# Score pairs in groups of two with a borrowed hidden bank, the second token transpose in two banks, and the norm of batch 1 moved ahead

## The reference

```python
x = x + xattn(layernorm(x), ctx, ctx)          # block-banded softmax, blocks of 64, out @ Wo.T
xn = layernorm(x)
top1 = argmax(softmax(xn @ gate_w.T))          # one of two experts per token
routed = sum_e relu(mask_e * xn @ w1[e] + b1[e]) @ w2[e] + b2[e]
x = x + routed + relu(xn @ sw1 + sb1) @ sw2 + sb2
```

## Time and profile before

| | us |
|---|---|
| median of 3 runs (944.99 to 947.7) | 946.83 |
| the profiled execution | 948.77 |
| its span | 946.6 |
| PE busy in the span | 807.7 (85%) |
| DVE, ACT, POOL busy | 598.4, 493.3, 420.3 |

### The profile page before, as it was taken

How to read it: one execution, slowest core, us unless ns; L and a number is a source line. 1 busy time by engine, 2 the same in 40 slices (tenths; PEclk the granted TensorE clock), 3 DMA queues, 4 the chain that set the end, 5 groups by cost and what they waited for, 6 DMA issues and landing times.

```text
span 946.6 us, 23198 instructions
## 1 busy us (share of the span) xinstructions
PE 807.7 (85%) x7862; PEld 670.6 (71%) x7862; DVE 598.4 (63%) x1226; ACT 493.3 (52%) x1108; POOL 420.3 (44%) x773
## 2 busy tenths in 40 slices
PE   3277877899998999898999989898989899988984
PEld 3146656586877868685968778686869596868884
DVE  3767584676758575776767575757577676646331
ACT  2373444436465555546464646455564646465542
POOL 3644324334344453635445544445363554455401
PEclk8587998979999999999999999999999999999998
DMA  8657232244435244344454453534434444414720
GB/s 269 172 150 252 78 102 67 76 137 142 151 110 185 88 147 149 107 148 136 135 153 144 128 172 95 172 110 133 152 115 137 152 133 137 142 46 134 253 83 23
DMA packets 97386, 128.17 MB, mean 135 GB/s; under 512 B 14655, under 2 KB 82623, under 8 KB 97088
## 3 DMA queue, kind: packets, MB, share of 16 engines
q1 hardware_dynamic: 89760, 107.89, 37.3%
q0 software_dynamic: 6624, 18.95, 5.9%
q10 hardware_dynamic: 960, 0.79, 0.4%
HBM read 90.80 MB, written 37.04 MB: 135 GB/s over the span
## 4 chain that ended last, share of the span: by engine, by line
PE 58%; DVE 15%; DMA 12%; ACT 6%; SPq 3%; issue 3%; POOL 1%; ACTq 1%; POOLq 0%; DVEq 0%
PE hid L502 19%; PE acc L671 13%; PE nd L596 10%; DVE T L1144 5%; DMA QP<-scratch_m 5%; PE work L580 4%; DMA scratch_m<-mT 3%; PE work L624 3%; PE work L502 2%; PE work L555 2%; DVE nmax L1125 2%; PE work L610 2%; DVE T L1141 2%; ACT h L925 1%; DVE Xs L1078 1%
## 5 line engine op out<-in xcount | busy, mean ns | idle before, releaser
L1404 POOL TENSOR_TENSOR hl<-h,hh 128x256 fp32r<-128x256 f32 x228 | 169.0, 744 | 351.2 <-ACT hh L925 351.1
L908 ACT ACTIVATE PT<-work 128x512 f32<-128x512 f32 x256 | 139.3, 600 | 58.4 <-PE work L580 55.8
L1144 DVE RECIPROCAL T<-nd 128x256 f32<-128x256 f32 x64 | 112.1, 1752 | 77.8 <-PE nd L596 74.0
L925 ACT ACTIVATE h<-hid,bias 128x256 f32<-128x256 f32 x144 | 69.0, 480 | 117.1 <-PE hid L502 117.1
L502 PE MATMUL hid<-Xs,W 128*128 128x256 f32 x816 | 115.1, 296 | 10.8 <-DVE Xs L1078 10.8
L502 PEld LDWEIGHTS hid<-Xs,W 128*128 128x128 f32 x816 | 105.1, 199 | 17.7 <-issue 10.8
L671 PE MATMUL acc<-w_hi,hh 128*128 128x256 f32 (+1 forms) x528 | 110.7, 292 | 0.0
L671 PE MATMUL acc<-w_lo,hh 128*128 128x256 f32 (+1 forms) x528 | 105.4, 281 | 0.0
L502 PE MATMUL hid<-Xr,W 128*128 128x256 f32 x768 | 105.3, 287 | 0.0
L596 PE MATMUL nd<-PT,V 128*32 128x256 f32 x1024 | 83.3, 398 | 25.4 <-DVE T L1146 22.5
L1125 DVE TENSOR_REDUCE nmax<-work 128x8 f32<-128x512 f32 x128 | 82.3, 685 | 35.1 <-PE work L555 35.0
(11 more groups left out here) (184 smaller groups left out, 1511.5 us busy)
## 6 DMA issues: line engine op xcount, KB each, us to landing
W<-w1q SPq DMA_DIRECT2D x64, 512.0 KB, 5.6
KP<-scratch_k SPq DMA_DIRECT2D x192, 64.0 KB, 2.3
QP<-scratch_q SPq DMA_DIRECT2D x180, 64.0 KB
scratch_k<-T SPq DMA_DIRECT2D x16, 512.0 KB, 3.5
scratch_q<-T SPq DMA_DIRECT2D x16, 512.0 KB, 3.3
yt<-yq SPq DMA_DIRECT2D x17, 260.0 KB, 2.8
xt<-xq SPq DMA_DIRECT2D x17, 256.0 KB, 3.8
xin<-x SPq DMA_DIRECT2D x16, 256.0 KB, 3.8
```

Of the source, the lines that this page charges most:

```text
L908: nc.scalar.activation(PT[:, j % 4].rearrange("p t q -> p (t q)"), work[:, BANK[("st", j)], :], ACT.Exp).then_inc(sem["exp_done"], 1)
L925: last = nc.scalar.activation(dst, hid[:, u % 2, a, :], ACT.Relu, bias=bias[:, 2 * u + a:2 * u + a + 1])
L1144: nc.vector.reciprocal(T[:, p, :], nd[:, p % 2, 1, :]).then_inc(sem["inverted"], 1)
L1404: nc.gpsimd.tensor_tensor(R(hl[:, u % 2, a]), h32[:, u % 2, a], hh[:, u % 2, a], ALU.subtract).then_inc(sem["hl_done"], 1)
```

## The change

- **Groups of two pairs.** `scores_t` of two pairs run back to back, then a fill, then both `values`. A group has four score jobs but `work` three banks; the fourth job goes into a half of `hid` (`score_bank`, `SPARE`), and waits there for the ReLU of the unit that lay in it (`relued`). Now the odd pair of each group is guessed, and the fills are one to a group: `shared_down` 3, `tile_up` 1, `tile_down` 0, `tile_up` 2. On ACT each group is four exponentials, in the first two groups a ReLU of the tile, then the guess.
- **x2T in two banks.** The token transposes of channel half 0 go to `work`, of half 1 to `hid`; each half has its own semaphore step, ACT and DVE split each half, and `shared_up` 0 waits for the second half only in its middle.
- **Shared units one place later.** `shared_down` 0 moves behind visit 2, 1 behind visit 3, 2 behind `tile_tokens`, 3 into the first group; ACT's ReLU of unit 3 moves behind the copy of the maxima, and DVE's `finish_shared` behind the next query projection.
- **attention_out** is done by channel half: 32 products of 64 columns in place of 16 of 128; the first half waits for four divides only.
- **Start.** Loads of batch 1 stand ahead of the key and query round trips, its statistics and norm ahead of the first maxima, the first weight splits of ACT ahead of its query loads.
- **Iterations 1 and 2**: ACT's `table_relu` moves from ahead of the last guess to behind it.
- **Tail.** The tile transposes of the last batch come two units later on PE, and SP reads the two row numbers before it waits for the padding.

```diff
-FILLED = {0: ("up", 1), 2: ("down", 0), 4: ("up", 2)}
-GUESSED_EARLY, GUESSED = (1, 3, 5, 7), (2, 3, 6, 7)
+FILLED = {1: ("up", 1), 2: ("down", 0), 3: ("up", 2)}
+GROUPS = PAIRS // 2
+SPARE = (1, 0, 0, 1)
+GUESSED_EARLY, GUESSED = (1, 3, 5, 7), (1, 3, 5, 7)
...
+        def score_bank(j):
+            if j % 4 == 3:
+                return flat(hid[:, SPARE[j // 4]])
+            return work[:, BANK["st", j], :]
+        def relued(i, group):
+            if type(i) is int and i == 0:
+                return None
+            if type(i) is int and i < 3:
+                return shared_unit(i - 1, UNITS - 1)
+            if group == 0 and type(i) is int and i == BATCH - 1:
+                return tile_unit(i - 2, 1)
+            if group == 0:
+                return shared_unit(i - 1, UNITS - 1)
+            return tile_unit(i - 2, SPARE[group])
+        def x2T_chunk(c):
+            return work[:, BANK["x2T", 0], 0:SEQ] if c == 0 else hid[:, 1, 0, :]
...
+            load_x(1)
+            load_ctx(1)
             bounce(0, "k_lo", kn, scratch_k, "first_k_bounced")
...
-            load_ctx(1)
-            load_x(1)
             iteration(0, False, False, True)
...
+            rows = [sp.value_load(left[0:1, e:e + 1], min_val=0, max_val=QROWS - TILE) for e in range(2)]
             for u in range(UNITS):
...
             sp.wait_ge(sem["padded"], 64)
-            rows = [sp.value_load(left[0:1, e:e + 1], min_val=0, max_val=QROWS - TILE) for e in range(2)]
...
             def scores_t(i, p, more):
-                banks = [claim(i, ("st", 2 * p + s), more) for s in range(2)]
+                banks = [score_bank(j) if j % 4 == 3 else claim(i, ("st", j), more) for j in (2 * p, 2 * p + 1)]
+                if p % 2:
+                    free = relued(i, p // 2)
+                    if free is not None:
+                        pe.wait_ge(sem["relu_done"], 2 * free + 2)
+                    if p > 1:
+                        pe.wait_ge(sem["exp_done"], HEADS * i + 2 * p - 2)
...
-                pe.wait_ge(sem["t_done"], PAIRS * (i + 1))
...
+                for c in range(DC):
+                    pe.wait_ge(sem["t_done"], PAIRS * i + 4 * c + 4)
+                    for r in range(NBLK):
+                        queries = slice(BLOCK * r, BLOCK * r + BLOCK)
+                        for q in range(4):
+                            mm = nc.tensor.matmul(bank[32 * q:32 * q + 32, c, queries], hsum[:, r, :],
+                                                  T[:, 4 * c + q, queries], start=True, stop=True)
...
+                if type(i) is not int or i > 0:
+                    pe.wait_ge(sem["relu_done"], 2 * last_odd(i) + 2)
+                transposes(bank, xhat2, "x2T_full", apart=hid[:, 1, 0, :])
...
                     ranks(n, claim(i, ("rk", 0), tile=tile))
-                    shared_down(n, 0)
                 visit(i, 2, more)
                 if shared:
+                    shared_down(n, 0)
                     shared_up(n, 2)
+                visit(i, 3, more)
+                if shared:
                     shared_down(n, 1)
-                visit(i, 3, more)
                 if tile:
                     shared_up(n, 3)
-                    shared_down(n, 2)
                 maxima(i)
...
-                    shared_down(n, 3)
+                    shared_down(n, 2)
...
-                scores_t(i, 0, more)
-                for p in range(PAIRS):
-                    if more or p != 0:
-                        fill(n, m, tile, p, expert)
-                    if p + 1 < PAIRS:
-                        scores_t(i, p + 1, more)
-                    values(i, p)
+                for group in range(GROUPS):
+                    scores_t(i, 2 * group, more)
+                    scores_t(i, 2 * group + 1, more)
+                    if more or group > 1:
+                        fill(n, m, tile, group, expert)
+                    values(i, 2 * group)
+                    values(i, 2 * group + 1)
...
                 high(i, "mT_full", work[:, BANK[("mT", 0)], 0:P], mT[:, 0, :], "mT_hi")
+                if tile:
+                    shared_relu(n, UNITS - 1)
...
+                for group in range(GROUPS):
+                    for j in range(4):
+                        exps(i, 4 * group + j)
+                    if tile and more and group < 2:
+                        tile_relu(m, group)
...
+                    guess_inverse(i, 2 * group + 1)
+                    if shared and not tile and group == 3:
                         table_relu(i - 1)
...
+            norm1_stats(1)
             for n in range(EARLY_PIECES):
                 if by_vector(n):
                     split_low(n)
+            norm1_apply(1)
             for j in range(4):
                 maximum(0, j)
```

More of the change, by code:

```diff
@@ L646, in ranks, with up @@
                                  skip_group_check=True).then_inc(sem["rk_full"], 1)
-            def up(g, u, weights, tokens):
+            def up(g, u, weights, tokens, second=None):
                 if type(g) is not int or g >= 2:
@@ L654, in up @@
                                        [(weights[:, u, 0, c, cols], weights[:, u, 1, c, cols]) for c in range(DC)],
-                                       [(tokens[:, 0, c, :], tokens[:, 1, c, :]) for c in range(DC)])
+                                       [(tokens[:, 0, c, :], tokens[:, 1, c, :]) for c in range(DC)],
+                                       second if a == 0 else None)
                 mm.then_inc(sem["hid_full"], 1)
@@ L767, in iteration @@
                 if tile:
+                    if not more:
+                        shared_down(n, 3)
                     tile_up(m, 0)
@@ L940, in tokens_high @@
             def tokens_high(i):
-                high(i, "x2T_full", work_bank("x2T"), Xs[:, 0], "x2_hi")
+                for c in range(DC):
+                    high(DC * i + c, "x2T_full", x2T_chunk(c), Xs[:, 0, c], "x2_hi")
             def table_relu(e):
@@ L967, in iteration @@
                     splits(i, u + 1)
[L968 removed]
+                    if shared and u < UNITS - 1:
                         shared_relu(n, u)
@@ L983, in iteration @@
                     front_q(i + 1)
-                if tile:
+                if tile and not more:
                     tile_relu(m, 0)
-                    if not more:
-                        tile_relu(m, 1)
-                elif shared:
+                    tile_relu(m, 1)
+                elif shared and not tile:
                     shared_relu(n, UNITS - 1)
@@ L1037, in _ @@
             projection_high(3)
+            for n in range(EARLY_PIECES):
+                split_high(n)
             act.wait_ge(sem["first_q_bounced"], 16)
@@ L1191, in shared_low @@
             def shared_low(i):
-                low(i, "x2_hi", work_bank("x2T"), Xs[:, 0], Xs[:, 1], "x2_lo")
+                for c in range(DC):
+                    low(DC * i + c, "x2_hi", x2T_chunk(c), Xs[:, 0, c], Xs[:, 1, c], "x2_lo")
             def tile_low(n, src, tokens=Xr):
```

101 lines of the change are left out of this document (47 added, 54 removed).

## The result

| | before | after |
|---|---|---|
| median of 19 runs each, same chip (us) | 945.23 | 936.68 |
| lowest and highest | 941.85, 951.81 | 927.67, 943.35 |
| ratio, 95% interval | | 0.9894 (0.9868 to 0.992) |
| the profiled execution, its span | 948.77, 946.6 | 933.05, 931.1 |

The ratio is of fast runs alone; two of after's 19 runs, 942.81 and 943.35, count as slow. It makes 946.83 into 936.8: 10 us gained, not 25. The time lies inside the range, but the size of the gain is wrong. ("After" is the changed kernel's run, in text and tables.) The profiled execution of after is one of the quicker ones: 15.5 us of span less than before. The sum is taken apart by places that both records have. "Tile unit" is `tile_up` 3, behind attention_out.

The account below looks back on a forecast made before the run. PE was taken to bound the steady iterations, 51.5 us each with 4.3 standing. Gains of 18 steady, 4 start, 0 for iterations 1 and 2 and 3 at the end made 25: 946.83 to 922 us, range 905 to 942.

Parts of the forecast that it names:

- The steady iteration: Iterations 3 to 14: 1.55 us less each, from earlier first scores and attention_out; twelve make 18, bounds 7 to 26.
- visit 2: In each steady iteration, PE now arrives before DVE finishes visit 1's maxima: 1.45 us of new standing.
- the clock's term: In the steady sum, the granted clock was taken to stay at 1.00, with no cost for a fall.
- rival 2: Visit 2's wait makes the clock fall in each steady iteration, losing 2.4 us each: 951 us; above 947, chance 0.10.
- its sign of being wrong: Steady part: a granted clock under 0.98 would show the prediction wrong, as would exponentials releasing `values` or no visit 2 wait.
- rival 1: Steady pairs stay bound by ACT and DVE, slipping 0.3 us a group: 936 us; 930 to 943, chance 0.20.
- Start: Before the first scores: batch 1's statistics and norm moved, 4 us gained, 3.2 to 5.6, lower bound 2.
- Iterations 1 and 2: Gains of 1.4 + 0.6 before the pairs, lost to 2 to 3 us more table wait: net 0, -5 to +4.
- rival 3: Visit 2's new wait is absent because DVE reaches the maxima sooner: 903 us; with larger start gain, 898 to 912, chance 0.10.
- rival 4: Nothing changes: the start loses its gain to the DMA queue, the table the steady part's; chance 0.05.
- Tail: After iteration 14: 1.2 us from reading row numbers ahead of a wait, with iteration 15's gain 3 us in sum.
- The 1.7 of iteration 15: Iteration 15's shift and pairs were to gain 0.8 + 0.9 us, part of the 3 us for the end.

Follow-up runs that it names:

- after_5: The changed kernel itself without any edit, run again beside other variants on one chip; 0.9861 of the kernel before.
- before_v2: The kernel before with one edit, visit 2 put ahead of `shared_down` 0; 1.0127 of the kernel before.
- norm_later: The changed kernel with DVE's `norm1_apply` moved behind visit 1's maxima, PE's order untouched; 0.9706 of the kernel before.

## Why the forecast was wrong, point by point

- **The steady iteration was right.** Forecast 1.55 less, measured 1.75 where the clock held. The wait for Xs is gone (at 497.07 PE starts without one); visit 2 waits 1.21, forecast 1.45, with DVE's maxima as releaser, but in two pieces, 0.52 ahead of its first half and 0.69 ahead of its second, where one was forecast; the shift chain leaves 0.39, forecast 0.45; no wait stands ahead of `values`. The wait ahead of the second half of attention_out is 1.46, forecast 0.6: the last quotient ends 485.50 + 1.48 - 466.19 = 20.8 us after the first scores, the upper end of the 20.25 to 20.7, with a last step of 1.48 (0.92 in the earlier trace rows), and PE is there after 19.4:

```profile
485.50 1.48 DVE L1194 SCALAR_TENSOR_TENSOR T<-check,T 128x256 f32<-128x256 f32 x1
```

- **attention_out goes by columns.** Its second half takes 487.62 - 487.04 = 0.58 us for 32 pieces, 18 ns each on average. That is near the 0.5 of time by columns. The floor of about 25 ns between starts that the Trainium skill gives (TensorE: Matmul & The Clock Gate, "Wait — 56ns, not 53.3ns?") makes it 0.8, as an estimate. The measurement decides against the floor for products that fill a quarter of the output partitions each.
- **The step that failed is the clock's term.** The sum of a steady iteration, 1.55 and twelve times that, keeps the granted clock of before, 1.00, for a kernel with a new standing of its own in visit 2: a fall of the clock costs nothing in it. The fall stands in rival 2 alone, all or nothing, with a chance of 0.10 for one in each iteration at 2.4 us. The argument against it was that four to five waits an iteration leave the clock alone now and that the standing falls in sum. The first was read from a mean that hides the one fall of before; the sum is not what counts, since two waits of 0.5 and 0.7 with only a visit's few products between them were enough, in 16 of 22 periods. A mixed case was the result: in the record of after 11 x 1.75 us gained, 6 x 1.7 lost; in that of after_5 ten falls, at a granted clock of 0.97 over the 11 periods, which is below the 0.98 that the prediction named as its sign of being wrong. The rule of the Trainium skill that the prediction weighed (TensorE: Matmul & The Clock Gate, "A second HAM failure mode: psum-queue depth-cycling") spoke for this: the waits of visit 2 are for banks of PSUM, and the clock swings behind them.
- **The range held by luck.** 936.8 lies in the 930 to 943 of rival 1, pairs bound by ACT and DVE, and no such wait is there.
- **Start: -4 forecast, -4.2 at the first maxima,** -3.4 behind attention_out. What follows in iteration 0 was not seen: SP's stores now go ahead of the last weight load. The prediction asked what the loads at the start would collide with in the DMA engines, and not what SP does behind the scores.
- **Iterations 1 and 2: net 0 forecast, -1.1 measured** with iteration 0's rest in it. The table's wait is 2.07 longer (2.94 against 0.87), forecast 2 to 3.
- **Tail: -3 forecast, -1.1 measured.** The reading of the row numbers was on the chain that ended last, as the prediction took it, and its 1.2 is won: behind the padding's DMA the load of `xt` now follows after 0.17 us, where 1.4 lay between them before.

```profile
876.73 5.96 DMA yq<-T
...
882.86 6.46 DMA xt<-xq
```

  But that load takes 6.46 in place of 5.04. The 1.7 of iteration 15 did not come through either: the padding's DMA is issued 82.6 us behind the tile unit of iteration 14, before 82.1, since the scatter of rows to `xq` ahead of it starts 0.8 sooner and takes 4.81 in place of 3.62. What remains of the gain comes from the clock: behind the load PE needs 41.7 us to the end, before 43.4, and its first unit ran at a granted clock of 0.55 before and runs at 1.00 now. Why the two transfers got slower stays open.
- **Rivals 1, 3 and 4** are out: no exponential releases `values` in a steady iteration, visit 2 does wait, and the start and the steady part both gain.

## What to carry to other kernels

When an order on PE is changed, ask not only how much waiting is left but how it lies: two short waits with little work between them halved the clock here for 3.4 us at a time, where nearly all longer single waits did not. Price such a wait as its own length plus a share of a fall, and look for a unit of work that can stand in front of it; here one line moved was worth 2%. When one stage gets quicker, follow every queue that waits for it, also those that only store.

## What the runs showed of the hardware that was not expected

- The granted clock fell in some of the periods and not in others with the same instructions and, to 0.02 us, nearly always the same waits. Each fall goes to half. At visit 2 of after and after_5 it starts 0.5 to 1.6 us after PE is back at work and costs 1.7 us; behind a wait for a quotient (before, before_v2, norm_later) it starts 0.1 to 0.8 us after it and costs 0.6 to 1.4.
- The falls keep a time of their own. These are three of the five that follow one another in the record of after (windows over the fall alone):

```profile
503.27:506.68 3.41, 3.41 (x18) 3.41 (x17) 1.20 (x2) 0.00 (x0) 0.82 (x1) 0.50 0.00 0
554.47:557.88 3.41, 3.41 (x18) 3.41 (x17) 1.43 (x3) 0.00 (x0) 1.04 (x1) 0.50 0.00 0
...
708.07:711.48 3.41, 3.41 (x17) 3.41 (x18) 1.97 (x4) 0.00 (x0) 1.59 (x2) 0.50 0.00 0
```

  All five start 51.20 us apart, while the disturbed periods take 51.3 to 51.4. Against the instructions each fall therefore comes about 0.2 us sooner than the last, from 16.2 down to 15.4 us behind the start of attention_out's second half; the sixth would come at 15.3, and there is none. In after_5 five come 15.8 to 15.4 behind that place, then a period has none, then five come at 16.4 to 15.9. So it matters when a wait comes, and not only how long it is; and since a disturbed period is about as long as the step from fall to fall, disturbed periods follow one another. This is read from two records; no run moved the waits in time on purpose, and what sets the falls' time is not shown.
- Length alone does not tell. A single wait of 1.45 to 1.72 ahead of attention_out's second half stands in all 99 periods of the nine records that guess pair 5, and only one such wait (1.67, in norm_later) had a fall behind it; yet 0.5 + 0.7 around a visit had 16 of 22. What makes that difference is open.
